# Weighted values of 16 heads on four quarters of the TensorE array, in two PSUM banks

## The chip, the cores and the metric

The kernel runs on one core of a Trainium2 chip. The metric is the device time of one execution in microseconds. TensorE (PE) multiplies, ScalarE (ACT), VectorE (DVE) and GpSimd (POOL) do the rest, and SyncE (SP) issues the transfers.

## What is computed

A decoder of two layers over 64 sequences of 64 tokens, 128 features each, in float32: 4096 tokens, which the kernel holds as 32 tiles of 128 tokens, two sequences to a tile. The parts are, in order: a delta-rule attention, a cross-attention of 16 heads with 8 features, six layers of local attention and feed-forward, then a causal attention of 16 heads with 8 features, a gated cross-attention and a mixture of 16 experts. The step of the change is the weighted sum of values of the two attentions with 16 heads, cut to what matters:

```python
attn = softmax(scores)                       # b, h, q, k: 16 heads, 64 x 64 per sequence
out = jnp.einsum('bhqk,bhkd->bhqd', attn, v) # d = 8
out = out.transpose(0, 2, 1, 3).reshape(B, T, D) @ Wo
```

## The kernel before

**Stages.** The work is in three stages, written by hand with one stream of instructions for each engine. The first ("AB", 32 units, one for each tile) holds the delta rule and the first cross-attention. The middle one ("C1" and "C2") holds the six layers. The last ("DE", 32 units) holds the causal attention, the gated attention and the experts.

**Order.** A unit is cut into phases with short names. `AB_ORDER` and `DE_ORDER` (lines 78 to 96) give for each engine the order of phases in a slot, with a lag: `u5` runs phase `u` of the tile five back. Several tiles are so in work at once, and one slot finishes one tile. `schedule` (line 391) makes each engine's sequence of it; every engine executes its own in that order, and waits on semaphores that count the phases of the others. In the first stage TensorE's slot is V b1 s O u a2 o b2 T w a3 b3 G a4 D b4 v x X p1 t q Z a1 W y p0 J, where the phases of one slot belong to different tiles.

**Phases around the change.** In AB: `J` is the projection of the delta rule into a bank, read by ACT (`J`, `j`) and DVE (`R`, then `Q`). `V` is the last product of the block inverse; DVE `U` waits for it. `O` is the delta rule's output; ACT squares it, DVE `so`, `s2`, POOL `ro` and DVE `N` normalise it, and TensorE `o` transposes that. `a1` to `a4` and `b1` to `b4` are products of sixteen 32x32 blocks; ACT copies `a` out for `b`, DVE subtracts `b` (`d`) and transposes (`t`). `s` makes the scores; the exponentials are transposed by `p0`, `p1` and copied to `PT`. `u` (line 672) calls `weighted16` (line 695), DVE `r` and `n` divide by the sum that stands in each head's ninth column, TensorE `t` transposes, ACT `t` copies to `OT`, and TensorE `y` multiplies by the output weights. In DE the same steps are `u`, `r`, `n`, `t`, and then `w` for the product with `D_Wo`; `h` and `o` with a letter are the two products of an expert, `G` to `C` the weights of the gated attention.

**The weighted values before.** For each of 16 heads and each of the two sequences: one product with a 64x64 stationary operand (the transposed exponentials) and 9 moving columns (8 values and a one). Sequence 0 lies in partitions 0 to 63 and its result goes to partitions 0 to 63, sequence 1 in 64 to 127 and goes there; so two of the array's four 64x64 quarters are used, in turn. All 144 columns of results lie in one bank.

**Banks.** PSUM has eight banks. `take` (line 410) deals them in a rotation in the order of TensorE's phases: each phase gets the next bank, a phase in `AB_PAIRS` or `DE_PAIRS` gets two and begins at an even one (`turn += turn % wide` skips one where needed). Before a phase writes, TensorE waits for the phases that empty the bank's last user (`u.after`); `AB_EMPTIED` (line 142) names them: `"J": ("dve Q",)`, `"u": ("dve n",)`. In the middle stage the rotation has six banks and two are fixed.

Of the kernel before, what the change touches and what calls it, by code (L numbers as in the profile page):

```python
# [146 lines left out]
for _l in "1234":  # L147
    AB_EMPTIED.update({"a" + _l: ("act a" + _l,), "b" + _l: ("dve d" + _l,)})

AB_PAIRS = ("G", "s")  # L150

DE_EMPTIED = {
# [4 lines left out]
}  # L157
for _x in EXPERTS:
    DE_EMPTIED.update({"h" + _x: ("act k" + _x,), "o" + _x: ("dve x" + _x,)})
DE_PAIRS = ("s", "G")  # L160


class Unit:
# [53 lines left out]
def build(nc, din, out, stages=("A", "B", "C", "D", "E", "F"), depth=DEPTH):  # L217
    with ExitStack() as ctx:
# [237 lines left out]
        def pair(u, c):  # L456

            return PS[u.bank["G"] // 2][:, :].rearrange("p (n c) -> p n c", n=2)[:, :, c:c + 256].rearrange("p n (g j) -> p n g j", j=64)

        def program(ab, c1, c2, de, name):  # L460
            for u, ph in schedule(name):
                {"AB": ab, "C1": c1, "C2": c2, "DE": de}[u.kind](u, ph)
# [102 lines left out]
        def _(te):  # L565
            w = Waits(te, sems)

            def mm(o, l, r, start=True, stop=True, check=True):
                return te.matmul(o, l, r, start=start, stop=stop, skip_group_check=not check)  # L569
# [14 lines left out]
            def pe_ab(u, ph):  # L584
# [27 lines left out]
                elif ph[0] == "a":  # L612
                    n = int(ph[1])
                    w.wait_ge(*u.on("dve", f"t{n - 1}"))
                    w.wait_ge(*u.on("pool", "l"))
                    o = blocks16(K, b.BT[:, 128 * n - 128:128 * n], b.D)
                elif ph[0] == "b":
                    w.wait_ge(*u.on("act", "a" + ph[1]))
                    o = blocks16(K, b.E, b.X) if ph[1] < "4" else blocks16(K, b.X, b.E)
                elif ph == "Z":  # L620
                    w.wait_ge(*u.on("dve", "R"))
                    w.wait_ge(*u.on("dve", "d4"))
                    o = blocks16(K, b.E, b.R)
                elif ph == "W":
                    w.wait_ge(*u.on("act", "C"))
                    w.wait_ge(*u.on("act", "Z"))
                    for h in range(4):
                        c = slice(32 * h, 32 * h + 32)
                        for q in (0, 64):
                            o = mm(K[q + 32:q + 64, c], b.CX[q:q + 32, c], b.Z[q:q + 32, c])  # L630
                elif ph == "V":
                    w.wait_ge(*u.on("act", "W"))
                    for h in range(4):
                        c = slice(32 * h, 32 * h + 32)
                        for r in (slice(32, 64), slice(96, 128)):
                            o = mm(K[r, c], b.E[r, c], b.W[r, c])
                elif ph == "O":
                    w.wait_ge(*u.on("dve", "q"))
                    w.wait_ge(*u.on("dve", "U"))
                    for h in range(4):  # L640
                        c = slice(32 * h, 32 * h + 32)
                        for q in (slice(0, 64), slice(64, 128)):
                            o = mm(K[q, c], b.QM[q, 64 * h:64 * h + 64], b.Z[q, c])
                elif ph == "o":
                    w.wait_ge(*u.on("dve", "N"))
                    o = tr(K[:, 0:128], b.ON)
                elif ph == "w":
                    w.wait_ge(*u.on("act", "o"))
                    w.wait_ge("const", 3)
                    o = mm(K[:, 0:128], b.oT, woA[:, :])  # L650
                elif ph == "x":
                    w.wait_ge(f"c{t // 4}", 16)
                    tr(K[:, 128:256], c_sb[:, t, :])
                    w.wait_ge(*u.on("dve", "xn2"))
                    o = tr(K[:, 0:128], b.xnB)
                elif ph == "v":
                    w.wait_ge("k_b", 16 * len(SETS["b"]))
                    w.wait_ge(*u.on("act", "x"))
                    o = mm(K[:, 0:128], b.xc[:, 128:256], T["XWv"][:, :])
                elif ph == "q":  # L660
                    w.wait_ge("k_b", 16 * len(SETS["b"]))
                    w.wait_ge(*u.on("act", "x"))
                    mm(K[:, 0:128], T["XWq"][:, :], b.xc[:, 0:128])
                    o = mm(K[:, 128:256], T["XWk"][:, :], b.xc[:, 128:256])
                elif ph == "s":
                    w.wait_ge(*u.on("act", "q"))
                    o = scores(u.bank[ph], b.qT, b.k4, 512)
                elif ph[0] == "p":
                    w.wait_ge(*u.on("act", "e" + ph[1]))
                    for i in range(4):  # L670
                        o = tr(K[:, 128 * i:128 * i + 128], b.P[int(ph[1])][:, 128 * i:128 * i + 128])
                elif ph == "u":
                    for m in ("v", "p0", "p1"):
                        w.wait_ge(*u.on("act", m))
                    o = weighted16(K, b.PT, b.V9)
                elif ph == "t":
                    w.wait_ge(*u.on("dve", "n"))
                    o = tr(K[:, 0:128], b.On)
                elif ph == "y":
                    w.wait_ge(*u.on("act", "t"))  # L680
                    o = mm(K[:, 0:128], b.OT, T["XWo"][:, :])
# [10 lines left out]
                        o = mm(half(bank[k + g // 2][par:par + 64, :], bb), qT[r, 64 * bb:64 * bb + 64], half(km[r, :], bb))  # L692
                return o

            def weighted16(K, PT, V):
                for h in range(16):
                    c = 128 * (h % 4) + 64 * (h // 4 % 2)
                    for q in (slice(0, 64), slice(64, 128)):
                        o = mm(K[q, 9 * h:9 * h + 9], PT[h // 8][q, c:c + 64], V[q, 9 * h:9 * h + 9])
                return o  # L700

            def pe_bank(u, ph):
# [105 lines left out]
            def pe_de(u, ph):  # L808
# [22 lines left out]
                elif ph == "u":  # L831
                    w.wait_ge(*u.on("dve", "v"))
                    for m in ("p0", "p1"):
                        w.wait_ge(*u.on("act", m))
                    o = weighted16(K, b.PT, b.V9)
                elif ph == "t":
                    w.wait_ge(*u.on("dve", "n"))
                    o = tr(K[:, 0:128], b.On)
# [70 lines left out]
        def _(se):  # L909
# [21 lines left out]
            table("natural_log_exp_and_others")  # L931
            w.wait_ge("k_a", 16 * len(SETS["a"]))

            def act_ab(u, ph):
                b, sm = ab_bufs(u), ab_bufs(u).sm
                K = bank[u.bank[{"j": "J", "C": "G", "D": "G"}.get(ph, ph)]] if ph[0] != "e" else None
# [18 lines left out]
                elif ph[0] == "a":  # L955
                    o = copy(b.X, K[:, 0:128])
                elif ph == "Z":
                    o = copy(b.Z, K[:, 0:128])
                elif ph == "W":
                    for q in (slice(32, 64), slice(96, 128)):  # L960
                        o = copy(b.W[q, :], K[q, 0:128])
                elif ph == "O":
                    o = act(b.SQ[:, 0:128], K[:, 0:128], ACT.Square)
                elif ph == "o":
                    o = copy(b.oT, K[:, 0:128])
                elif ph == "x":
                    o = copy(b.xc, K[:, 0:256])
                elif ph == "v":
                    w.wait_ge("const", 2)
                    o = copy(b.V9[:, :].rearrange("p (h d) -> p h d", d=9)[:, :, 0:8], K[:, 0:128].rearrange("p (h d) -> p h d", d=8))  # L970
                elif ph == "q":
                    w.wait_ge("k_b", 16 * len(SETS["b"]))
                    copy(b.qT, K[:, 0:128])
                    for i in range(4):
                        o = act(b.k4[:, 128 * i:128 * i + 128], K[:, 128:256], ACT.Copy, scale=T["hm8"][:, i:i + 1])
                elif ph[0] == "p":
                    o = copy(b.PT[int(ph[1])], K)
                elif ph == "t":
                    o = copy(b.OT, K[:, 0:128])
                o.then_inc(u.name("act", ph, sems), 1)  # L980

            def act_c1(u, ph):
# [90 lines left out]
            def act_de(u, ph):  # L1073
# [19 lines left out]
                elif ph in ("p0", "p1"):  # L1093
                    o = copy(b.PT[int(ph[1])], K)
                elif ph == "t":
                    o = copy(b.oT, K[:, 0:128])
                elif ph == "xc":
                    w.wait_ge("k_d", 16 * len(SETS["d"]))
                    copy(b.xc, K[:, 0:256])
# [45 lines left out]
        def _(ve):  # L1145
# [20 lines left out]
            def dve_ab(u, ph):  # L1166
# [86 lines left out]
                    w.wait_ge(*u.on("dve", f"s{n}"))  # L1253
                    o = red(sm[:, 3, 8 * n:8 * n + 8], g64(b.P[n]), ALU.max)
                elif ph == "r":
                    o = ve.reciprocal(sm[:, 4, 0:16], K[:, 0:144].rearrange("p (h d) -> p h d", d=9)[:, :, 8])
                elif ph == "n":
                    w.wait_ge(*u.on("dve", "r"))
                    o = tt(b.On.rearrange("p (h d) -> p h d", d=8), K[:, 0:144].rearrange("p (h d) -> p h d", d=9)[:, :, 0:8],
                           bc(sm[:, 4, 0:16], 8), ALU.mult)  # L1260
                o.then_inc(u.name("dve", ph, sems), 1)

            def newton(u, o, a, t, i):
# [125 lines left out]
            def dve_de(u, ph):  # L1389
# [59 lines left out]
                elif ph in ("c0", "c1"):  # L1449
                    o = ts(b.P[int(ph[1])], bank[u.bank["s"] + int(ph[1])], 20.0, -20.0, ALU.min, ALU.max)  # L1450
                elif ph == "r":
                    o = ve.reciprocal(sm[:, 4, 0:16], K[:, 0:144].rearrange("p (h d) -> p h d", d=9)[:, :, 8])
                elif ph == "n":
                    w.wait_ge(*u.on("dve", "r"))
                    o = tt(b.On.rearrange("p (h d) -> p h d", d=8), K[:, 0:144].rearrange("p (h d) -> p h d", d=9)[:, :, 0:8],
                           bc(sm[:, 4, 0:16], 8), ALU.mult)
                elif ph == "w":
                    w.wait_ge(*u.on("pool", "bo"))
                    o = stt(x, K[:, 0:128], 0.5, x, ALU.mult, ALU.add)
# [312 lines left out]
```

## Time and profile before

| | us |
|---|---|
| median of 3 runs | 4253.59 (4252.46 to 4254.8) |
| the profiled execution | 4263.92 |
| its span, first to last instruction | 4262.1 |
| TensorE busy | 4071.3 (96%) |
| ScalarE busy | 3488.6 (82%) |
| VectorE busy | 3291.7 (77%) |
| GpSimd busy | 2653.4 (62%) |
| mean granted TensorE clock | 0.965 |

The times of phases below come from the profiled execution, which took 10.3 us (0.24%) more than the median. Busy is the time in which at least one instruction of the engine was in work; overlapping ones count once. Weight loads (PEld) and products (PE) are separate rows of TensorE; every float32 product appears as two records of each. The granted clock is 1.00 at 2.4 GHz and 0.50 at 1.2 GHz, so a mean between them says how the stretch was divided.

### The profile page before, as it was taken

To read this page: it belongs to the slowest core of one execution; us is meant where nothing else is said; L and a number is where in the kernel's file an instruction comes from. 1 tells how busy PE (TensorE), PEld (TensorE's weight loads), DVE (VectorE), ACT (ScalarE), POOL (GpSimd) and SP (SyncE) were. 2 spreads that over 40 slices of the span, in tenths; PEclk is the share of its full clock that TensorE was granted. 3 is DMA by queue.
4 is the path that set the end of the run, shared out by engine and by line. 5 is a ranking of instruction groups with operands and counts; after the bars stand their busy time and mean duration, and the time that the engine had idled before them with its cause. 6 is when DMAs were issued, how large, how long until landed. Compare 5 with 4: busy or idle time off the path is not lost.

```text
span 4262.1 us, 149492 instructions
## 1 busy us (share of the span) xinstructions
PE 4071.3 (96%) x61520; PEld 3074.8 (72%) x61520; DVE 3291.7 (77%) x9529; ACT 3488.6 (82%) x10059; POOL 2653.4 (62%) x2246
## 2 busy tenths in 40 slices
PE   7999989999999999999999999999999799999999
PEld 5777756666667666667666666676666588888889
DVE  4666578998888888888888888888888467767765
ACT  3455569999999999999999999999999356666665
POOL 3444467887777777777777777777777233333331
PEclk8888889999999999999999999999999789999999
DMA  3000000000000000000000000000000100000000
GB/s 105 4 4 4 4 2 4 5 4 5 30 3 4 4 30 4 4 4 4 30 4 5 5 30 4 5 3 9 27 10 9 30 2 4 4 4 4 4 4 7
DMA packets 65248, 46.34 MB, mean 11 GB/s; under 512 B 29220, under 2 KB 63032, under 8 KB 63800
## 3 DMA queue, kind: packets, MB, share of 16 engines
q1 hardware_dynamic: 64568, 36.78, 3.0%
q8 instruction: 487, 7.98, 0.8%
q14 instruction: 193, 1.58, 0.1%
HBM read 28.48 MB, written 2.10 MB: 7 GB/s over the span
## 4 chain that ended last, share of the span: by engine, by line
PE 41%; ACT 34%; DVE 8%; issue 2%; POOL 0%; ACTq 0%
PE ps L569 34%; ACT BIG L921 15%; ACT BIG L913 12%; PE ps L573 7%; DVE BIG L1149 3%; ACT ps L913 3%; ACT L928 2%; DVE sm L1160 2%; DVE BIG L1154 1%; ACT sm L921 1%; DVE BIG L1157 1%; DVE y_sb L1154 0%; DVE BIG L1153 0%; ACT XS L913 0%; POOL BIG L1591 0%
## 5 line engine op out<-in xcount | busy, mean ns | idle before, releaser
L569 PE MATMUL ps<-WB,BIG 128*128 128x128 f32 (+2 forms) x8576 | 1940.8, 363 | 53.4 <-DVE BIG L1157 47.7
L913 ACT ACTIVATE BIG<-ps 128x512 f32<-128x512 f32 (+6 forms) x3168 | 1518.4, 536 | 461.6 <-PE ps L573 277.8
L1591 POOL TENSOR_TENSOR BIG<-BIG,sm 128x512 f32<-128x512 f32 (+1 forms) x864 | 1221.3, 1425 | 563.6 <-DVE sm L1342 330.0
L569 PEld LDWEIGHTS ps<-WB,BIG 128*128 128x128 f32 (+1 forms) x8576 | 1154.3, 192 | 378.8 <-issue 224.7
L1591 POOL TENSOR_TENSOR BIG<-BIG 128x512 f32<-128x512 f32 x768 | 969.4, 1279 | 146.5 <-DVE BIG L1149 146.5
L1160 DVE TENSOR_REDUCE sm<-BIG 128x8 f32<-128x512 f32 (+3 forms) x1472 | 871.3, 610 | 157.8 <-ACT BIG L921 154.6
L573 PEld LDWEIGHTS ps<-t_ident,BIG 128*128 128x128 f32 x6016 | 731.3, 146 | 325.8 <-issue 167.8
L573 PE MATMUL ps<-t_ident,BIG 128*128 128x128 f32 x6016 | 888.0, 282 | 68.3 <-DVE BIG L1149 28.9
L569 PEld LDWEIGHTS ps<-BIG 64*64 64x64 f32 (+2 forms) x37888 | 617.4, 132 | 336.6 <-ACT BIG L913 78.3
L569 PE MATMUL ps<-BIG 64*64 64x64 f32 (+4 forms) x37888 | 737.2, 226 | 52.7 <-ACT BIG L913 18.6
L1594 POOL TENSOR_TENSOR sm<-sm,halfn 128x1 f32<-128x1 f32 (+2 forms) x336 | 290.5, 871 | 752.0 <-DVE sm L1153 419.8
L921 ACT ACTIVATE BIG<-ps,sm 128x64 f32<-128x64 f32 (+1 forms) x3104 | 694.4, 377 | 14.2 <-DVE sm L1160 10.5
L1149 DVE TENSOR_TENSOR BIG<-ps,rc 128x512 f32<-128x512 f32 x768 | 525.4, 684 | 195.6 <-ACT BIG L921 194.9
L569 PE MATMUL ps<-BIG,WB 128*128 128x128 f32 (+2 forms) x2624 | 597.1, 352 | 2.4 <-ACT BIG L921 1.4
L921 ACT ACTIVATE BIG<-ps 128x512 f32<-128x512 f32 (+1 forms) x832 | 514.7, 628 | 78.9 <-PE ps L569 75.5
L1149 DVE TENSOR_TENSOR BIG<-ps,rs 128x256 f32<-128x256 f32 x1536 | 570.8, 412 | 0.0
L569 PEld LDWEIGHTS ps<-BIG,WB 128*128 128x128 f32 (+1 forms) x2624 | 362.5, 193 | 94.0 <-issue 83.4
L921 ACT ACTIVATE BIG<-ps,t_F_b 128x128 f32<-128x128 f32 x1024 | 324.1, 375 | 83.5 <-PE ps L569 82.7
L1160 DVE TENSOR_REDUCE sm<-ps 128x8 f32<-128x512 f32 (+1 forms) x416 | 266.3, 640 | 72.0 <-PE ps L569 68.4
L913 ACT ACTIVATE ps<-t_bandm 128x512 f32<-128x512 f32 x384 | 266.6, 694 | 0.0
L928 ACT ACT_TABLE_LOAD x187 | 239.9, 1283 | 4.1 <-PEq L1763 0.7
L1157 DVE SCALAR_TENSOR_TENSOR x_sb<-ps,BIG,x_sb 128x128 f32<-128x128 f32 x512 | 177.0, 346 | 77.3 <-PE ps L569 67.4
(119 smaller groups left out, 2913.7 us busy)
## 6 DMA issues: line engine op xcount, KB each, us to landing
WB<-in_Wqkv SPq DMA_DIRECT2D x6, 1536.0 KB, 7.3
XS<-y_sb SPq DMA_DIRECT2D x96, 63.0 KB
y_sb<-in_ctx SPq DMA_DIRECT2D x16, 256.0 KB, 3.2
WB<-in_Wo SPq DMA_DIRECT2D x6, 512.0 KB, 9.0
x_sb<-in_x SPq DMA_DIRECT2D x8, 256.0 KB, 5.2
WB<-in_F_W SPq DMA_DIRECT2D x1, 2048.0 KB, 8.7
WB<-in_F_W SPq DMA_DIRECT2D x8, 256.0 KB, 4.9
out<-x_sb SPq DMA_DIRECT2D x8, 256.0 KB, 2.3
```

Of the source, the lines that this page charges most:

```text
L569: return te.matmul(o, l, r, start=start, stop=stop, skip_group_check=not check)
L573: return te.transpose(o, i, ident[0:n, 0:n])
L913: return se.activation(o, i, ACT.Copy)
L921: return se.activation(o, i, f, **kw)
L928: se.preload_act_table_set(name)
L1149: return ve.tensor_tensor(o, a, b, op)
L1154: return ve.tensor_scalar(o, a, s1, s2, op0, op1)
L1157: return ve.scalar_tensor_tensor(out=o, in0=a, scalar=s, in1=b, op0=op0, op1=op1)
L1160: return ve.tensor_reduce(o, a, AX, op, negate=negate)
L1591: return pe_.tensor_tensor(o, a, b, op)
L1594: return pe_.tensor_tensor(o, a, halfn[:, 0:n], ALU.pow)
```

## The change

`weighted16` takes the bank's number instead of the bank. It goes over eight pairs of heads (`j` and `j + 8`); heads 0 to 7 write to the first bank as before, heads 8 to 15 to the second bank with the two halves of the partitions exchanged, so that the four products of a pair use the four quarters. `u` is added to both lists of pairs. DVE `r` and `n` read the two banks through `weighted`. In the normalised result the columns 64 to 127 (heads 8 to 15) have the two sequences exchanged; after the transpose these are the partitions 64 to 127, and `restore` on ScalarE puts them back with three copies instead of one. The orders of the phases stay.

```diff
-AB_PAIRS = ("G", "s")
+AB_PAIRS = ("G", "s", "u")
-DE_PAIRS = ("s", "G")
+DE_PAIRS = ("s", "G", "u")
+        def weighted(u):
+
+            return PS[u.bank["u"] // 2][:, :].rearrange("p (n c) -> p n c", n=2)[:, :, 0:72].rearrange("p n (h d) -> p n h d", d=9)
...
-                    o = weighted16(K, b.PT, b.V9)
+                    o = weighted16(u.bank[ph], b.PT, b.V9)
...
-            def weighted16(K, PT, V):
-                for h in range(16):
-                    c = 128 * (h % 4) + 64 * (h // 4 % 2)
-                    for q in (slice(0, 64), slice(64, 128)):
-                        o = mm(K[q, 9 * h:9 * h + 9], PT[h // 8][q, c:c + 64], V[q, 9 * h:9 * h + 9])
+            def weighted16(k, PT, V):
+
+                for j in range(8):
+                    c = 128 * (j % 4) + 64 * (j // 4)
+                    for n in range(2):
+                        for bb in range(2):
+                            q, r, v = slice(64 * bb, 64 * bb + 64), slice(64 * (bb ^ n), 64 * (bb ^ n) + 64), 72 * n + 9 * j
+                            o = mm(bank[k + n][r, 9 * j:9 * j + 9], PT[n][q, c:c + 64], V[q, v:v + 9])
...
+            def restore(o, K):
+
+                copy(o[0:64, :], K[0:64, 0:128])
+                copy(o[64:128, 0:64], K[64:128, 64:128])
+                return copy(o[64:128, 64:128], K[64:128, 0:64])
...
-                    o = copy(b.OT, K[:, 0:128])
+                    o = restore(b.OT, K)
...
-                    o = ve.reciprocal(sm[:, 4, 0:16], K[:, 0:144].rearrange("p (h d) -> p h d", d=9)[:, :, 8])
+                    o = ve.reciprocal(sm[:, 4, 0:16].rearrange("p (n h) -> p n h", n=2), weighted(u)[:, :, :, 8])
...
-                    o = tt(b.On.rearrange("p (h d) -> p h d", d=8), K[:, 0:144].rearrange("p (h d) -> p h d", d=9)[:, :, 0:8],
-                           bc(sm[:, 4, 0:16], 8), ALU.mult)
+                    o = tt(b.On.rearrange("p (n h d) -> p n h d", n=2, d=8), weighted(u)[:, :, :, 0:8],
+                           sm[:, 4, 0:16].rearrange("p (n h) -> p n h", n=2).unsqueeze(3).broadcast_to([128, 2, 8, 8]), ALU.mult)
```

The last stage has the same edits for its `u`, `r`, `n` and `t`.

## Rows read from the trace of the kernel before

**Rows 1.** The page: busy time by engine, and the granted clock over 40 slices
```profile
PE 4071.3 (96%) x61520; PEld 3074.8 (72%) x61520; DVE 3291.7 (77%) x9529; ACT 3488.6 (82%) x10059; POOL 2653.4 (62%) x2246
...
PEclk8888889999999999999999999999999789999999
```

**Rows 2.** Table by stretch, first and last stage: us, busy by engine, clock, DMA
```profile
76.07:531.73 455.66, 422.22 (x13333) 342.79 (x13330) 279.77 (x1058) 227.65 (x781) 197.53 (x195) 0.83 0.02 4
...
3500.00:3900.00 400.00, 377.70 (x4458) 352.06 (x4458) 279.66 (x1269) 247.38 (x841) 130.37 (x165) 0.99 0.02 5
```

**Rows 3.** Waits in the first stage, then in the last: total, times, longest
```profile
DVE BIG L1149 <- PE ps L569: 135.8, 51, 5.6
...
PE ps L569 <- DVE BIG L1157: 35.5, 24, 1.9
```

**Rows 4.** Timeline of VectorE in one slot: start, us, operation, idle before
```profile
208.52 0.59 DVE L1149 TENSOR_TENSOR BIG<-BIG,ps 32x128 f32<-32x128 f32 x2 [5.16 <-PE ps L569]
...
212.13 0.69 DVE L1149 TENSOR_TENSOR BIG<-ps,sm 128x256 f32<-128x256 f32 x2
...
212.13 0.41 DVE L1149 TENSOR_TENSOR BIG<-ps,sm 128x256 f32<-128x256 f32 x1
```

**Rows 5.** Timeline of TensorE in the same slot, behind `u`: a2, o, b2, a3, b3
```profile
212.13 0.47 PE L569 MATMUL ps<-BIG 32*32 32x32 f32 x32
212.96 0.45 PE L573 MATMUL ps<-t_ident,BIG 128*128 128x128 f32 x1 [0.36 <-DVE BIG L1149]
213.34 0.65 PE L569 MATMUL ps<-BIG 32*32 32x32 f32 x32
...
215.18 0.65 PE L569 MATMUL ps<-BIG 32*32 32x32 f32 x32
216.23 0.28 PE L569 MATMUL ps<-BIG 32*32 32x32 f32 x4 [0.40 <-ACT BIG L913]
```

**Rows 6.** Timeline of the last stage: oH, w, copy t, r
```profile
3613.02 0.71 PE L569 MATMUL ps<-WB,BIG 128*128 128x128 f32 x4 [1.15 <-DVE BIG L1157]
...
3623.29 0.46 PE L569 MATMUL ps<-t_D_Wo,BIG 128*128 128x128 f32 x2
...
3622.93 0.28 ACT L913 ACTIVATE BIG<-ps 128x128 f32<-128x128 f32 x1 [0.47 <-PE ps L573]
...
3621.19 0.26 DVE L1452 RECIPROCAL sm<-ps 128x16 f32<-128x16 f32 x1 [1.12 <-PE ps L569]
```

**Rows 7.** Timeline of weight loads: O, `u`, `u`, and the middle stage's `y`, `y` with `s`
```profile
209.69 0.54 PEld L569 LDWEIGHTS ps<-BIG 64*64 64x64 f32 x16 [0.39 <-issue]
...
210.16 1.95 PEld L569 LDWEIGHTS ps<-V,BIG 64*64 64x64 f32 x64
...
3619.11 1.94 PEld L569 LDWEIGHTS ps<-V,BIG 64*64 64x64 f32 x64
...
2003.28 1.02 PEld L569 LDWEIGHTS ps<-BIG 64*64 64x64 f32 x64 [0.76 <-ACT BIG L921]
...
2013.58 1.96 PEld L569 LDWEIGHTS ps<-BIG 64*64 64x64 f32 x128 [0.76 <-ACT BIG L913]
```

**Rows 8.** Timeline of TensorE in a slot at full clock: a3 and b3
```profile
232.02 0.45 PE L569 MATMUL ps<-BIG 32*32 32x32 f32 x32
232.88 0.45 PE L569 MATMUL ps<-BIG 32*32 32x32 f32 x32 [0.41 <-ACT BIG L913]
```

**Rows 9.** Table by stretch: three slots, then a part of the last
```profile
227.76:242.49 14.73, 13.20 (x484) 10.53 (x481) 9.92 (x39) 8.21 (x28) 7.09 (x8) 1.00 0.02 3
242.49:258.94 16.45, 15.46 (x484) 12.62 (x480) 10.08 (x39) 8.12 (x28) 7.09 (x8) 0.79 0.02 4
210.16:227.76 17.60, 16.64 (x484) 13.58 (x480) 10.08 (x39) 8.10 (x28) 7.09 (x8) 0.71 0.01 4
...
212.60:223.00 10.40, 9.64 (x234) 7.94 (x238) 6.08 (x24) 4.70 (x15) 4.26 (x5) 0.51 0.01 3
```

**Rows 10.** Timeline of ScalarE: the two copies of phase W
```profile
239.28 0.55 ACT L913 ACTIVATE BIG<-ps 32x128 f32<-32x128 f32 x2
```

More of the change, by code:

```diff
@@ L834, in pe_de @@
                         w.wait_ge(*u.on("act", m))
-                    o = weighted16(K, b.PT, b.V9)
+                    o = weighted16(u.bank[ph], b.PT, b.V9)
                 elif ph == "t":
@@ L1095, in act_de @@
                 elif ph == "t":
-                    o = copy(b.oT, K[:, 0:128])
+                    o = restore(b.oT, K)
                 elif ph == "xc":
@@ L1451, in dve_de @@
                 elif ph == "r":
-                    o = ve.reciprocal(sm[:, 4, 0:16], K[:, 0:144].rearrange("p (h d) -> p h d", d=9)[:, :, 8])
+                    o = ve.reciprocal(sm[:, 4, 0:16].rearrange("p (n h) -> p n h", n=2), weighted(u)[:, :, :, 8])
                 elif ph == "n":
                     w.wait_ge(*u.on("dve", "r"))
-                    o = tt(b.On.rearrange("p (h d) -> p h d", d=8), K[:, 0:144].rearrange("p (h d) -> p h d", d=9)[:, :, 0:8],
-                           bc(sm[:, 4, 0:16], 8), ALU.mult)
+                    o = tt(b.On.rearrange("p (n h d) -> p n h d", n=2, d=8), weighted(u)[:, :, :, 0:8],
+                           sm[:, 4, 0:16].rearrange("p (n h) -> p n h", n=2).unsqueeze(3).broadcast_to([128, 2, 8, 8]), ALU.mult)
                 elif ph == "w":
```

## The prediction

> **What bounds the kernel now.** I read the page first: TensorE is busy 96% of the span and its clock row has 8s in the first six of 40 slices and a 7 and an 8 at the 32nd and 33rd [rows 1]. So the program is three stages with different limits, and the clock is part of them in the first and the last. The table by stretch has these two [rows 2]: in the first stage (28 slots, from one `u` to the next, 455.66 us) TensorE is busy 93% at a mean clock of 0.83; in the last stage TensorE is busy 94% at 0.99. The change touches only the first and the last stage. The middle one runs nothing of it, and its bank rotation (six banks, single turns) keeps the same distances, so I cost it at nothing.
>
> In the first stage the busy share deceives. The list of waits has VectorE waiting 135.8 us for TensorE [rows 3], so they take turns in part. One slot in order of time shows why. VectorE stands idle 5.16 us, gets the product of `V` at 208.52 and then works without a gap for 4.3 us (phases U, ss, d1, y, b, t1, s1, so, be, s2, R, s0, Q, N) until 212.82 [rows 4]. TensorE runs b1, s, O, `u`, a2 beside it and then waits 0.36 us for N before the transpose `o` [rows 5]. So `u` has cover there: even if it were free, `o` would start at 212.96, as now. The slot's length is set by that VectorE chain, by the chain of small steps after it, and by the clock.
>
> The last stage is different: after one wait per slot, ended by the DVE phase C (1.15 us at 3613.02; the waits give 35.5 us in 24), TensorE's phases stand end to end, `u` among them [rows 3, 6]. A shorter `u` is paid out there.
>
> **The change, part by part.**
>
> *The weighted values.* Before, 32 products of 64x64 by 9 columns go to two diagonal quarters; each fp32 product leaves two records, so 64 records take 1.95 us of weight loads (1.94 in the last stage), about 29 ns each [rows 7]. After, the same 64 records cycle through four quarters. The trace has that pattern already: the middle stage's `y` has 64 records of 64x64 on four quarters in 1.02 us, and a `y` with the next tile's `s` behind it 128 in 1.96, so `s` 64 in 0.94 [rows 7]; that is 14 to 16 ns a record though 64 columns move instead of 9. I take 1.02 us, a gain of 0.93 per `u`. If the narrow moving side made a difference the bound above is today's 1.95, below it `s`'s 0.94.
> The Trainium skill has two rules against this. "TensorE: Matmul & The Clock Gate" (section on why 56 ns and not 53.3) says that the start-to-start distance never falls below about 25 ns; by it 64 records need 1.6 us and the gain is 0.35. "TensorEngine Tiling (Array Packing)" (Gotcha 1: PSUM Pressure) says that different row tiles can't use one PSUM bank at once, and the new order sends both row halves to the same bank in pairs. The rows of `s` speak against both: it has the same pairs per bank, at under 15 ns.
>
> *Two banks instead of one.* This is the part that decides. `take` deals banks in turn, and a phase in the list of pairs begins at an even bank. From `J` on the PE order is J, V, b1, s (pair), O, u. If J has bank 1, V has 2, b1 3, s 4 and 5, O 6; `u` as a pair must skip 7 and gets 0 and 1. Bank 1 is J's, and J's bank counts as emptied only by the DVE phase Q (AB_EMPTIED). A slot takes 27 banks, one more for each of the three pairs and two skipped ones, 32 in all, a multiple of 8, so this repeats in every slot. I have 28 slots in which J of a later unit precedes `u` so. Q is the last but one of the VectorE chain: it begins at 212.13 and takes 0.41, so ends at 212.54, while `u` began at 210.16 [rows 4, 7]. N ended at 212.82 and the `o` that waited for it started at 212.96 [rows 4, 5], 0.14 later; so `u`, now at 210.16, will start at 212.66 or so, 2.5 us later, with TensorE idle. Behind it queue a2, o, b2, T, w, a3. a2 starts 1.0 us after that, at 213.7 (now 212.13). From one blocks phase over ScalarE to the next takes 0.86 us at full clock (232.02 to 232.88, a3 to b3) and 1.05 at half (215.18 to 216.23) [rows 5, 8]. So b2 starts at 214.55 to 214.75, now 213.34: 1.2 to 1.4 us late. VectorE's d2 waits for b2 and everything after it follows, so nothing later takes the delay up, and V of the next slot, from which Q is counted, is late by the same. 28 x 1.3 = +36 us.
> The other new bank neighbours release earlier than their users start, by 0.9 us or more in the first stage except b3 (behind n, the two shift together). In the last stage the two banks of `u` are free in time; gT gets one that waits for xL, worth under 0.1 us and hidden in front of `w`.
>
> *The clock.* A slot at full clock lasts 14.73 us, one at mean 0.79 16.45, one at 0.71 17.60 [rows 9]. Mean 0.71 of 17.60 is 10.2 us at the lower level (1.2 GHz), and costs 2.87: 0.28 us per us. Over the 28 slots clock 0.83 gives 155 us at 1.2 GHz, 5.5 a slot, costing 16.27 - 14.73 = 1.54 [rows 2]. All 10.2 us lie in the stretch from 212.60 to 223.00, which is at 0.51 [rows 9]; so the clock fell right behind `u`: there nine-column products and then small blocks with gaps stand, the sparsest work of the slot. The change puts 2.5 us of idle TensorE in front of this. I expect each slot to fall, as the 0.71 ones do: 2.87 - 1.54 = +1.3 at most; with a part of the low time on the idle itself I take +1.1. 28 x 1.1 = +31 us. Bounds: 0 and +37, and, if the low time grew once more by as much as the 0.71 slot has over the 0.79 one (10.2 less 6.9 us), +27 on top.
>
> *The copy in three parts.* One copy of 128x128 takes 0.28 us [rows 6]. Two copies on other partitions than their neighbour's don't overlap: two of 32x128 take 0.55 [rows 10]. A third, narrower one adds 0.1 to 0.2. So 0.65 to 0.75 in place of 0.28, +0.4. In the last stage `w` (t_D_Wo, 3623.29) starts as soon as the copy of 3622.93 is done [rows 6]: the 0.4 stands on the path. In the first stage it stands ahead of X, Z, q, W on ScalarE; where these stand close W, for which V waits, comes later by 0.3 or so, where a gap stands between, by nothing. +0.1 a slot, +3 us (0 to +10).
>
> *VectorE's r and n* read the same number of elements through a pattern with one more level: 0 (0 to +0.1 us each, covered in both stages; `r` has 1.12 us of idle before it in the last [rows 6]).
>
> **Sum.** First stage 36 + 31 + 3 = +70. Last stage: -0.93 + 0.41 = -0.52 a slot for 31 slots, -16; bounds -29 (the copy hidden) to -8. Together +54. The profiled execution took 4263.92 us (span 4262.1), so it would show 4318; the median of the runs is 4253.59, so I forecast **4308 us**.
>
> **The rivals.**
> *The clock keeps its habit.* The bank wait is there, but falls are no more frequent: 36 + 3 - 16 = +23, 4277 us. For: TensorE does the same columns per slot. Against: a falling clock here follows sparse work, and idle is sparser. 0.12.
> *Four quarters bring nothing with nine columns.* `u` stays at 1.95 us by a floor per instruction or a turn-taking at the bank. Then a2 starts 0.93 later still: 28 x 0.93 = +26, and the last stage gives +13 in place of -16: 4308 + 55 = 4363. For: a diagonal product with 32 columns (O: 16 records in 0.54 us) has 27 ns per record against 29 with nine, so columns don't set it, and something else does. Against: the four-quarter rows [rows 7]. 0.07. By the 25 ns that the Trainium skill's page gives, some 60% of that would come.
> *Faster: the clock no longer falls.* Today's falls come right behind the 1.95 us of sparse `u`. If compact products stop the falls, a slot is 14.73 + 1.3 = 16.03 against 16.27: 28 slots bring -7, the copies +3, the last stage -16, in sum -20: 4234 us. It decides from the point at which time at 1.2 GHz is under about 4 us a slot. Against: the idle. 0.05.
> *The change does less than it says*: the wait for Q is met by luck in most slots and gains and losses balance, within 8.5 us of 4253.6. Against: a chain without a gap and a fixed rotation. 0.02.
> My forecast has 0.74.
>
> **How the numbers follow.** Forecast's own bounds: 4277 - 5 below (clock rival and a little of the last stage's gain), above 4308 + 6 (clock at its bound) + 7 (copies) + 8 (the last stage's least) and part of the still longer low time: 4343. That takes in the first rival; the others, 0.14, are outside. The measurement can tell about 0.2%, 8.5 us. Faster by more: 0.05; within: 0.02; slower: 0.93.
>
> **What would show it.** In the first stage: `u` preceded by about 2.5 us of TensorE idle, ended by the DVE phase Q, in nearly all slots; `u` about 1.0 us; the wait before `o` gone; slots of 18 to 19 us, mean clock near 0.72. In the last stage: slots shorter by 0.5 us, `w` waiting for the third copy, the wait for C unchanged. The forecast fails if J's bank is not the one that `u` gets, if Q is reached sooner than 2 us after O, or if the clock stays up.

## The result, and the profile after

The changed kernel takes 4353.57 us (median of 4 runs, 4352.22 to 4357.17), the kernel before 4253.35 beside it (4252.46 to 4254.8): a ratio of 1.0236, interval 1.0223 to 1.025, so 100 us slower. The profiled execution took 4357.17 us, span 4355.4, that is 93 us more than the profiled execution before. It was forecast slower, by 54 us and at most 89.

The page of the profile has TensorE a little busier in us and less busy in share, and a lower clock row in slices 2 to 6, which are the first stage (before: 8s there, [rows 1]):

```profile
PE 4095.9 (94%) x61520; PEld 3084.5 (71%) x61520; DVE 3296.3 (76%) x9529; ACT 3514.2 (81%) x10187; POOL 2653.5 (61%) x2246
...
PEclk8766678999999999999999999999999879999999
```

The table by stretch (us, busy of PE, PEld, DVE, ACT and POOL with counts, granted clock, DMA share, GB/s): the first stage from the first `u` to the 29th, one slot of it, that slot's parts, and 400 us of the last stage.

```profile
76.66:634.60 557.94, 471.63 (x13325) 384.11 (x13326) 279.05 (x1051) 237.20 (x836) 195.31 (x193) 0.68 0.01 3
216.82:236.94 20.12, 17.02 (x476) 13.88 (x477) 10.08 (x39) 8.52 (x30) 7.10 (x8) 0.67 0.02 4
...
214.40:216.80 2.40, 0.11 (x4) 0.00 (x0) 2.40 (x9) 0.28 (x1) 2.28 (x3) 0.85 0.00 0
...
216.85:224.00 7.15, 6.58 (x207) 5.44 (x207) 3.55 (x13) 2.19 (x6) 2.34 (x3) 0.50 0.02 6
224.00:230.00 6.00, 6.00 (x166) 5.32 (x164) 2.44 (x12) 2.94 (x12) 1.83 (x2) 0.52 0.01 4
230.00:236.90 6.90, 4.44 (x128) 3.10 (x118) 4.02 (x15) 3.40 (x13) 2.85 (x3) 0.97 0.01 2
...
3500.00:3900.00 400.00, 369.00 (x4372) 335.27 (x4372) 279.95 (x1261) 250.01 (x854) 135.91 (x172) 0.94 0.01 4
```

The first stage took 455.66 us at a clock of 0.83 [rows 2], now 557.94 at 0.68: all of the loss and more. VectorE's busy time there is the same (279.77 to 279.05), so nothing got longer on the engine that the slot waits for; the time is wait and clock. A mean clock of 0.67 in 20.12 us is 2 x 0.33 x 20.12 = 13.3 us at 1.2 GHz. The parts show where: the clock has already fallen in the 2.40 us in which TensorE has nothing to do ahead of `u` (0.85), and stays at 0.50 through `u` until some 13 us behind its start. Before, the low part began behind `u`, at 212.60, and ended at 223.00 [rows 9]. Over the stage, 15 of the 28 falls begin in the idle ahead of `u` (up to 0.8 us ahead of its start), 10 within 0.6 us behind its start and 3 behind it by 1.7; before, there were 19 falls, 18 of them 2.3 to 4.5 us behind the start of `u`.

The waits of TensorE over the first stage (what waited for what: us in total, times, longest) have a new first row; line 1162 is VectorE's product, of which phase Q is one:

```profile
PE ps L573 <- DVE BIG L1162: 63.2, 27, 2.5
PE ps L573 <- ACT BIG L920: 19.2, 49, 0.6
```

One slot in order of time (start, us, operation, idle before): VectorE from `U` to N, then TensorE's product and weight-load rows around `u`, at half clock, and the product row of `u` in another slot at full clock:

```profile
212.68 0.59 DVE L1162 TENSOR_TENSOR BIG<-BIG,ps 32x128 f32<-32x128 f32 x2 [5.45 <-PE ps L573]
...
216.29 0.69 DVE L1162 TENSOR_TENSOR BIG<-ps,sm 128x256 f32<-128x256 f32 x2
```
```profile
216.85 1.89 PE L573 MATMUL ps<-V,BIG 64*64 64x9 f32 x64 [2.34 <-DVE BIG L1162]
...
213.86 0.54 PEld L573 LDWEIGHTS ps<-BIG 64*64 64x64 f32 x16 [0.39 <-issue]
216.82 1.82 PEld L573 LDWEIGHTS ps<-V,BIG 64*64 64x64 f32 x64 [2.42 <-issue]
...
436.26 1.12 PE L573 MATMUL ps<-V,BIG 64*64 64x9 f32 x64 [2.33 <-DVE BIG L1162]
```

VectorE's chain is as it was [rows 4]: 4.3 us without a gap. O's weight loads end at 214.40, where `u` used to follow at once [rows 7]; now `u` starts at 216.82, 2.42 us later, as Q releases it. That holds in each of the 28 slots (2.28 to 2.61 us, 26 of them 2.41 or 2.42). At full clock `u` takes 1.02 to 1.1 us, at half clock 1.82; of the 28, 20 take over 1.6 us, 5 lie between, where the clock falls inside `u`, and 3 are at full clock.

In the last stage (TensorE, then ScalarE) `u`, the transpose `t`, the copies and `w` are these; [rows 6] and [rows 7] are their like before:

```profile
3723.20 1.12 PE L573 MATMUL ps<-V,BIG 64*64 64x9 f32 x64
...
3725.80 0.38 PE L577 MATMUL ps<-t_ident,BIG 128*128 128x128 f32 x2
3726.02 0.61 PE L573 MATMUL ps<-WB,BIG 128*128 128x128 f32 x4
3726.77 0.49 PE L573 MATMUL ps<-t_D_Wo,BIG 128*128 128x128 f32 x2
```
```profile
3726.11 0.61 ACT L920 ACTIVATE BIG<-ps 64x128 f32<-64x128 f32 x3 [0.47 <-PE ps L577]
```

The three copies take 0.61 us for 0.28, and `w` follows their end by 0.05. From the weight loads of `t` to those of `w` it takes 1.08 us, before 0.75. An ordinary slot went from 26.31 to 25.73 us.

Where the 93 us lie, stretch by stretch in the two traces and in those of the experiments below, each from the start of one `u` to the start of another (32 in each of the two stages); "low" is the time at 1.2 GHz in the stretch. "Middle" goes from the 29th `u` of the first stage to the first of the last, so it holds three slots of the first stage too (40.9 us before, 44.4 after):

| | first stage, `u` 1 to 29 | low | middle | last, `u` 1 to 5 | last, `u` 5 to 32 | low | span |
|---|---|---|---|---|---|---|---|
| before | 455.7 | 157 | 2827.8 | 100.3 | 728.3 | 17 | 4262.1 |
| after | 557.9 | 358 | 2830.6 | 100.5 | 716.4 | 24 | 4355.4 |
| e1_last_only | 452.1 | 140 | 2823.6 | 99.4 | 718.8 | 24 | 4244.0 |
| e2_pair_only | 587.4 | 369 | 2828.0 | 100.2 | 726.1 | 17 | 4393.5 |
| e9_pair_free | 464.8 | 157 | 2830.7 | 100.0 | 721.5 | 10 | 4266.5 |
| e3_other_banks | 466.6 | 184 | 2832.3 | 99.7 | 702.0 | 7 | 4249.5 |
| e4_filled_wait | 566.7 | 92 | 2836.9 | 99.9 | 705.0 | 10 | 4360.8 |
| e5_fill_ten | 502.8 | 92 | 2833.9 | 99.7 | 702.7 | 10 | 4291.3 |
| e6_before_filled | 452.9 | 89 | 2836.7 | 100.7 | 711.0 | 0 | 4252.4 |
| e7_banks_filled | 467.3 | 68 | 2831.5 | 97.5 | 706.2 | 10 | 4250.5 |
| e8_last_banks | 452.9 | 147 | 2837.0 | 99.2 | 685.1 | 0 | 4227.0 |

From the last `u` of the first stage to the first of the last, where the code is all but the same in all of them, the time differs by up to 11 us from one execution to another (2783.0 to 2794.1). The first stage of one and the same code took 455.7, 452.1 and 452.9 us (before, e1_last_only, e8_last_banks). So a difference of some 10 us between two spans says nothing, and one of 4 us in the first stage neither; a stage must be read by itself.

### The profile page after: what moved, and what is told of

Same layout as the page of the kernel before. It is cut to its first block, busy times and chain, and to the rows that moved or that the text cites. A ratio compares the mean times of both kernels' runs of the same rounds, so it can differ in the third digit from the quotient of the medians.

```text
span 4355.4 us, 149619 instructions
## 1 busy us (share of the span) xinstructions
PE 4095.9 (94%) x61520; PEld 3084.5 (71%) x61520; DVE 3296.3 (76%) x9529; ACT 3514.2 (81%) x10187; POOL 2653.5 (61%) x2246
## 4 chain that ended last, share of the span: by engine, by line
PE 39%; ACT 34%; DVE 7%; issue 2%; POOL 0%; ACTq 0%
PE ps L573 32%; ACT BIG L928 15%; ACT BIG L920 13%; PE ps L577 7%; DVE BIG L1162 3%; ACT ps L920 3%; ACT L935 2%; DVE sm L1173 2%; DVE BIG L1167 1%; ACT sm L928 1%; DVE BIG L1170 1%; DVE BIG L1166 0%; DVE y_sb L1167 0%; ACT XS L920 0%; POOL BIG L1604 0%
## 5 line engine op out<-in xcount | busy, mean ns | idle before, releaser
L920 ACT ACTIVATE BIG<-ps 128x512 f32<-128x512 f32 (+6 forms) x3296 | 1541.2, 523 | 535.2 <-PE ps L573 267.0
L577 PEld LDWEIGHTS ps<-t_ident,BIG 128*128 128x128 f32 x6016 | 742.4, 148 | 317.4 <-issue 166.1
L577 PE MATMUL ps<-t_ident,BIG 128*128 128x128 f32 x6016 | 904.7, 286 | 61.2 <-DVE BIG L1162 23.2
L573 PEld LDWEIGHTS ps<-BIG 64*64 64x64 f32 (+2 forms) x37888 | 639.9, 136 | 345.9 <-issue 103.3
L573 PE MATMUL ps<-BIG 64*64 64x64 f32 (+4 forms) x37888 | 762.6, 231 | 54.6 <-ACT BIG L920 23.0
L1162 DVE TENSOR_TENSOR BIG<-BIG,ps 128x128 f32<-128x128 f32 (+1 forms) x192 | 54.7, 285 | 261.8 <-PE ps L573 260.3
```

The source lines that it names most:

```text
L577: return te.transpose(o, i, ident[0:n, 0:n])
L920: return se.activation(o, i, ACT.Copy)
L1162: return ve.tensor_tensor(o, a, b, op)
```

## The experiments

Theory: the second bank of `u` is `J`'s, so `u` waits for Q; that wait costs once by itself and once more through the clock, and the last stage gains. Rivals: four-quarter products cost the first stage something themselves; the three copies do; the clock's part is only a companion, and the wait does it all.

**One stage alone.** The lines of the first stage are taken back, the last one keeps the change:

```diff
-AB_PAIRS = ("G", "s", "u")
+AB_PAIRS = ("G", "s")
...
-                    o = weighted16(u.bank[ph], b.PT, b.V9)
+                    o = old16(K, b.PT, b.V9)
...
-                    o = restore(b.OT, K)
+                    o = copy(b.OT, K[:, 0:128])
```

> The change in the last stage alone; the first stage is as before. Theory (the loss comes whole from the first stage, where u waits for the DVE phase Q): the last stage keeps its slot of 25.73 us against 26.31, so 4241 us (4236 to 4247). Rival (part of the loss is in the last or the middle stage, from new bank neighbours): above 4253.

Measured: 4237.0 us (4233.25 to 4245.78), ratio 0.9945 (0.9924 to 0.9966). The first stage is back at 452.1 us. The last stage alone makes the kernel faster, so the loss is the first stage's entirely.

**The pair alone.** The kernel before, with `u` in the first stage's list of pairs; products and copy stay, the second bank is dealt and not written:

```diff
-AB_PAIRS = ("G", "s")
+AB_PAIRS = ("G", "s", "u")
```

> The kernel before with one word more: u takes a pair of banks in the first stage and uses only the first of them; products, reads and copy as before. Theory (the bank that it shares with J makes the loss): u waits 2.4 us for Q in each slot, the clock falls for about 13 of 20 us, slots of 20 to 21 us, 4353 to 4375 us. Rival (four-quarter products or the copy in three parts make the loss): below 4275.

Measured: 4390.05 us (4385.02 to 4395.3), ratio 1.0304 (1.0282 to 1.0326). One entry in a list, with no instruction more, costs 136 us: more than the whole change. Its weight loads around `u`, and the row of that stretch in the table (clock third from the end):

```profile
206.93 3.52 PEld L569 LDWEIGHTS ps<-V,BIG 64*64 64x64 f32 x64 [2.35 <-issue]
210.47 0.51 PEld L569 LDWEIGHTS ps<-BIG 32*32 32x32 f32 x32
```
```profile
206.93:210.45 3.52, 3.49 (x64) 3.52 (x64) 0.95 (x3) 0.00 (x0) 1.33 (x2) 0.50 0.02 5
```

The same wait, and behind it the old `u` at 0.50, which takes 3.52 us and not 1.95, in 14 of the 28 slots. I had priced `u` at its full-clock duration; in these slots it isn't one, which fits with a run 15 us above what was expected. With four quarters `u` takes 1.82 us there, 1.7 less, and the first stage is 29.5 us shorter (557.9 for 587.4). So behind the wait the new products are a gain, and the wait is the loss.

**The wait away, the rest kept.** The whole change, but `u` in the first stage passes over two more banks, so that its pair is 2 and 3 in place of 0 and 1:

```diff
-            turn += turn % wide
+            turn += turn % wide + 2 * (ph == "u" and u.stage == "ab")
```

> The change whole, but u's pair in the first stage begins two banks further, so that its banks are those of V and b1, emptied by U and d1 before u starts, and not p0's and J's. Theory: no wait before u, the wait before o grows from 0.4 to 1.3 us instead, slots of 16.3 us or a little more as before, 4242 us (4230 to 4262). Rival (products and copies themselves cost in the first stage): above 4300.

Measured: 4250.61 us (4241.58 to 4265.9, 10 runs), ratio 0.999 (0.9972 to 1.0008). The first stage is 466.6 us, 91 less than after. Its weight loads of `u`, a2 and `o`:

```profile
239.95 0.14 PEld L573 LDWEIGHTS ps<-V,BIG 64*64 64x64 f32 x2
...
240.00 1.04 PEld L573 LDWEIGHTS ps<-V,BIG 64*64 64x64 f32 x62
242.13 0.34 PEld L573 LDWEIGHTS ps<-BIG 32*32 32x32 f32 x32 [1.09 <-DVE BIG L1170]
242.75 0.14 PEld L577 LDWEIGHTS ps<-t_ident,BIG 128*128 128x128 f32 x1 [0.27 <-DVE BIG L1162]
```
```profile
241.40 0.68 DVE L1170 SCALAR_TENSOR_TENSOR BIG<-ps,t_causm 128x512 f32<-128x512 f32 x1
```

`u` starts with O's last loads and is over in 1.04 us; but then a2 waits 1.09 for VectorE, and `o` starts 2.8 us after `u`, as before [rows 5, 7]. What `u` saves in this stage is idle time. The wait of a2 is for a bank once more: two banks further in the rotation it gets one of `s`'s, which VectorE's `s1` empties (the last row, done at 242.08). It moves neither `o` nor b2, which start 2.80 and 3.06 us after `u` (before 2.78 and 3.04). The run was expected at 4242 and lies inside its range; the stage isn't as long as before's, but 11 us longer, with 184 us at 1.2 GHz for 157.

**The pair without the wait.** To see whose those 11 us are: the pair-only kernel with the same passing over of two banks, so old products, old copy, no wait for Q.

```diff
-AB_PAIRS = ("G", "s")
+AB_PAIRS = ("G", "s", "u")
...
-            turn += turn % wide
+            turn += turn % wide + 2 * (ph == "u" and u.stage == "ab")
```

> e2_pair_only with the pair two banks further, as in e3_other_banks; products, reads and copies as before. Theory (of the 137 us that e2 lost all is the wait and its clock): 4247 to 4258 us, no wait before u. Rival (a pair more in the rotation costs by itself, through skipped banks): above 4270. Beside e3 (4250.6) and e1 (4237.0) it tells whether e3's first stage lost to its pair or to its products and copies.

Measured: 4269.64 us (4263.02 to 4286.08, 10 runs), ratio 1.0039 (1.0025 to 1.0053), 12 us above what was expected and at the edge of the rival that a pair more costs something by itself. The first stage takes 464.8 us, within 2 us of the 466.6 of the whole change on the same banks. So products and copies together change the first stage there by no more than such stages differ anyway. But the two stages don't lose in the same way. With the whole change the full-clock slots are those of before (14.6 to 14.9 us) and the low time is 27 us longer, worth 7.6 us at 0.28. Here the low time is that of before, the nine full-clock slots take 14.6 to 15.6 us (mean 14.9, before 14.7), and three slots take 19.6 to 20.4 us with 10.2 to 13.7 us low, for which 14.7 and 0.28 us per us give 17.6 to 18.5. TensorE's waits have a row that before's hardly has (0.5 us once):

```profile
PE ps L569 <- issue: 4.4, 8, 1.2
```

These eight idle times lie between two products of 32x32 blocks, none of them at a wait for a semaphore. What ended them the trace doesn't say, and it stays open.

**The wait filled.** The whole change with its wait; but between O and `u` TensorE multiplies the identity by itself into columns of `u`'s bank that nobody reads, first 18 and then 10 times. These products are no part of the computation. If the clock is a cost of its own, the kernel gets faster by added work.

```diff
                 for v, e, m in u.after[ph]:
-                    w.wait_ge(*v.on(e, m))
+                    if m != "Q" or ph != "u":
+                        w.wait_ge(*v.on(e, m))
+                if ph == "u":
+                    for i in range(18):      # second kernel: range(10)
+                        mm(bank[u.bank[ph]][:, 128:256], ident[:, :], ident[:, :])
+                for v, e, m in u.after[ph]:
+                    w.wait_ge(*v.on(e, m))
```

> The change whole, and 18 products of 128x128 without use (36 records of 128 columns, about 2 us at 2.4 GHz) written to u's first bank ahead of the wait for Q; u overwrites nothing that is read, its result is the same. The wait stays. Theory (of the loss about a third is the wait, two thirds the clock that it lets fall): granted clock near 1.0 in the first stage, slots of 16.1 us in place of 20.2, 4245 us (4238 to 4280). Rival (the wait itself costs the 100 us, the clock is a by-product): 4335 to 4365.

> As e4_filled_wait, with 10 useless products instead of 18. In e4 a record of these took 117 ns, so 36 held TensorE 4.2 us, 1.8 longer than the wait; 20 records are 2.3 us, just the wait of 2.4. Theory (about a third of the loss is the wait, the rest the clock): slots at full clock of 16.4 to 16.5 us, first stage 465 to 485 us in place of 558, 4262 to 4285 us. Rival (the wait itself costs the 100 us): 4335 to 4365.

Measured: with 18, 4353.26 us (4346.47 to 4362.61), ratio 1.0216 (1.0193 to 1.0238), far from the 4245 expected: the 36 records took 4.2 us, 1.8 more than the wait, so `u` came late by that, and a slot at full clock took 18.2 to 19.4 us. The low time had fallen from 358 to 92 us all the same. It was expected that the 36 records would take about 2 us; they leave TensorE 117 ns apart. With 10, 4283.02 us (4277.16 to 4293.14), ratio 1.0077 (1.0051 to 1.0103): 70 us faster than after, by nothing but work whose result is thrown away (in the traces 55 us of it lie in the first stage and 14 in the last, which runs the same code in both). Its rows, fill, `u` and b2 of one slot and the table of the slot before (clock 1.00), of this one (0.83), and of the stage (0.91):

```profile
174.83 2.50 PE L573 MATMUL ps<-t_ident 128*128 128x128 f32 x20
177.26 1.12 PE L573 MATMUL ps<-V,BIG 64*64 64x9 f32 x64
...
179.25 0.45 PE L573 MATMUL ps<-BIG 32*32 32x32 f32 x32 [0.24 <-ACT BIG L926]
```
```profile
158.53:174.83 16.30, 14.77 (x501) 12.05 (x497) 10.03 (x39) 8.46 (x30) 7.09 (x8) 1.00 0.02 4
174.83:194.59 19.76, 17.57 (x501) 14.42 (x497) 10.19 (x39) 8.47 (x30) 7.09 (x8) 0.83 0.01 3
76.50:579.30 502.80, 452.31 (x13889) 370.63 (x13886) 281.31 (x1058) 238.28 (x837) 197.35 (x195) 0.91 0.02 4
```

The fill reaches from 174.83 to 177.26, 2.43 us, exactly the wait. So the first row is a slot with the wait and without the clock: 16.30 us (14 such slots, 16.26 to 16.53 with a mean of 16.38, and one of 17.33) against 14.73 [rows 9]. The wait by itself, with what little the new products and copies add, costs some 1.65 us a slot, 28 x 1.65 = 46 us. After's slot of 20.12 us has 13.3 us low, so (20.12 - 16.30) / 13.3 = 0.29 us per us, the price that before's slots have. Of the first stage's 102 us the other 56 are the clock, and (358 - 157) x 0.28 gives the same 56. That rules out the rival that the wait does it all: with the wait kept, the first stage is 55 us shorter.

The stage itself missed its 465 to 485 us. Its 92 us at 1.2 GHz cost (502.8 - 28 x 16.38) / 92 = 0.48 us each: its 13 falls begin 6.0 to 8.4 us behind the start of `u`, in other phases than before's. So 0.28 is the price of the stretch around and right behind `u`. Whether the other phases make a us at 1.2 GHz dearer, or the fill, which leaves TensorE less idle time in the slot, isn't shown.

**Fillers in other places.** If low time costs 0.28 us per us, before's 157 us are worth 44 us. Two kernels put useless products ahead of phases that wait, one on the kernel before, one on the whole change with `u` on the other banks:

```diff
+                for i in range({"o": 1, "b3": 2, "a4": 1}.get(ph, 0)):      # second kernel: "o": 4, "b3": 1, "a4": 1
+                    mm(bank[u.bank[ph]][:, 0:128], ident[:, :], ident[:, :])
```

> The kernel before with useless 128x128 products in waits of the first stage: one ahead of o, two ahead of b3, one ahead of a4, each 0.23 us at 2.4 GHz, written to the phase's own bank and overwritten. Theory (the clock falls for sparse work and costs 0.28 us for each us at 1.2 GHz, 157 us of them in before's first stage): clock near 1.0, first stage 415 to 430 us in place of 456, 4212 to 4230 us. Rival (idle and order of work set the slots, the clock follows without cost): 4254 or above, since the products can only delay.

> e3_other_banks with useless products: four ahead of o, one ahead of b3, one ahead of a4. With u short and unhindered, o waits 1.2 us for N; four products (0.94 us) fit. Theory: clock near 1.0 in the first stage, slots of 14.8 us, first stage 415 to 425 us, and the last stage's gain of 12: 4200 to 4215 us. Rival (the shorter u brings nothing even so and the fill delays): 4240 or above.

Measured: 4244.06 us (4234.17 to 4254.21, 10 runs), ratio 0.9986 (0.9971 to 1.0002), and 4240.05 us (4235.58 to 4255.25), ratio 0.9982 (0.9965 to 0.9999). Both missed what was expected, by 14 and 25 us from the nearer end. The table rows of the first stage say why: the clock did rise, to 0.90 and 0.93 (before 0.83, [rows 2]), but the length didn't follow.

```profile
77.30:530.20 452.90, 437.71 (x13557) 354.64 (x13554) 281.83 (x1058) 227.89 (x781) 197.77 (x195) 0.90 0.02 4
```
```profile
74.70:542.00 467.30, 417.77 (x13671) 333.85 (x13669) 281.94 (x1058) 236.56 (x837) 197.48 (x195) 0.93 0.02 4
```

In the first, a slot at full clock takes 14.9 to 15.5 us for 14.7. In the second b2 starts 3.6 to 5.0 us after `u`, in place of 3.0 to 3.3 in e3_other_banks, behind the fillers, and eight records of them take 1.16 us at full clock and 2.08 at half. The four products ahead of `o` counted on a wait of 1.2 us for N; but a2 takes 1.0 us of it with its wait for `s1`, and `o` itself waits 0.3. Filling paid here in the 2.4 us ahead of `u`, where TensorE waits as long as the filler lasts, and not in waits of 0.3 us.

**The last stage's own bank waits.** With the last stage alone changed, one wait a slot is left there, that for C [rows 3]. Two phases pass over two banks:

```diff
+            turn += {"oH": 2, "p1": 2}.get(ph, 0) * (u.stage == "de")
             turn += turn % wide
```

> e1_last_only (change in the last stage alone), and in the last stage the rotation skips two banks ahead of oH and two ahead of p1. oH then no longer gets the bank of G that the DVE phase C empties; in the trace of before it waits 1.15 us for that in each slot, and C's value itself is wanted only three phases later. Theory (the wait for C is a bank wait like the one of u, of the rotation's making): oH and hL go ahead, slots shorter by 0.6 to 0.9 us, 4210 to 4222 us. Rival (the wait only moves to p1 or ct, which need POOL's and C's results): 4234 to 4240 as e1.

Measured: 4226.67 us (4224.9 to 4228.74), ratio 0.9932 (0.9906 to 0.9958), 5 us above what was expected and below what the rival gives; it is the fastest kernel of this study by its median, though its interval overlaps that of e1_last_only. The waits of TensorE from 3500 to 3900 us, of after and then of this kernel:

```profile
PE ps L573 <- DVE BIG L1170: 18.5, 13, 1.9
PE ps L577 <- POOL BIG L1604: 5.0, 2, 2.8
```
```profile
PE ps L578 <- ACT BIG L936: 7.4, 16, 0.5
```
```profile
3500.00:3900.00 400.00, 388.63 (x4759) 355.70 (x4759) 300.69 (x1355) 271.22 (x934) 138.64 (x173) 1.00 0.02 5
```

The wait for C was a wait for a bank. A slot is 25.36 us instead of 25.73 (two of 25.5 and 25.6), those of 26.45 and 28.1 are gone, the clock is 1.00, and 27 slots take 685.1 us for the 718.8 of e1_last_only. Of these 34 us only 17 show between the two spans, since the middle took 13 us more and what follows the last `u` 3, and 10 between the medians; why is open.

A kernel with four quarters and one bank was not tried. There the two row halves would write to the same partitions of one bank, and no run here shows whether that is safe.

## Why the prediction was wrong in size and right in mechanism

*Cover in the first stage, density in the last: right.* Without the wait the faster `u` brings the first stage nothing (e3_other_banks against e9_pair_free: 466.6 and 464.8 us; `o` starts 2.80 us after `u`, before 2.78); the last stage gains 0.58 us in an ordinary slot.

*`u` at 1.02 us: right at full clock* (1.02 to 1.09), so 16 ns per record where the Trainium skill ("TensorE: Matmul & The Clock Gate", on why 56 ns and not 53.3) has about 25 ns as the least distance. And two row halves in pairs on each bank run at that rate, where the Trainium skill ("TensorEngine Tiling (Array Packing)", Gotcha 1: PSUM Pressure) says that they can't use one bank at once. The measurement decides in both. But the term was taken at full clock, while behind the wait 20 of 28 `u` run at half clock wholly or nearly so (1.71 to 1.83 us).

*The bank: right in place and length, small in price.* `u` waits for Q in all 28 slots, by 2.42 us (2.5 forecast). In e5_fill_ten b2 starts 4.4 us after O's last load (179.25 against 174.83), in before's slots at full clock 3.0, so 1.4 later (1.2 to 1.4 forecast). The slot grows by 1.65 in place of 1.3 + 0.1 with the copies: 46 us in place of the 39 of both. Where the other 0.25 us come from is open.

*The clock: the step that failed.* I let each slot fall as before's worst slots do, 10.2 us low, and capped the term at +1.3 with 1.1 chosen. That took the place and length of the low stretch from the kernel before, while the change moves what goes ahead of them: the fall begins about where `u` starts, in 15 slots in the idle ahead of it, and no longer behind it, so the stretch holds `u` as well and lasts 13.3 us in the slot shown. Such a slot pays (13.3 - 5.5) x 0.29 = 2.3 us, and the mean of the 28 is 2.0, not 1.1. By the stage: 56 us where 31 stood. The case was in my bounds (the low time growing once more, +27), and I left most of it out of the range; with the whole of it the upper end would have been 4356 and held the time. The expected slots of 18 to 19 us at 0.72 were 20.2 at 0.67.

*The copies: near.* 0.61 us for 0.28, +0.33 on the path in the last stage (0.41 forecast). In the first stage they and the products together make 2 us when nothing waits for Q (3 forecast), less than the 4 us by which stages of the same code differ.

*The last stage: -12 in place of -16.* The ordinary slot gave more than forecast (0.58 for 0.52). But slots come in three lengths: before, of 27, 14 took 26.3 to 26.5 us, 8 took 27.0 and 5, with a fall of the clock, 28.7; after, 13 took 25.7, 7 took 26.4 and 7 took 28.1. So two slots more fell. In e3_other_banks, whose last stage is the same, 2 fell and the stretch takes 702.0 us for 716.4: that share is scatter between executions, not the change's; 27 ordinary gains of 0.58 are 16 us, the forecast.

*The sum.* First stage +102 for +70, last stage -12 for -16, middle +3 for 0: 93 in the profiled executions, 39 more than forecast. The +3 belong to the change too: the three slots of the first stage behind the 29th `u`, which no term of mine counted, grew from 40.9 to 44.4 us. The median moved by 100 since before's profiled execution lay 10 us above its median and after's 4.

*The rivals.* The clock's keeping its habit and the clock's no longer falling both fell by the 358 us low; four quarters bringing nothing fell by the 1.02 us; the wait being met by luck in most slots fell by the 28 waits in 28 slots.

## What to carry to other kernels

Where buffers are dealt in rotation, one entry wider is a new set of neighbours for every phase behind it: before such a change, list for each phase whose buffer it gets and when that one is emptied, in the trace of the kernel before. One false wait in front of a cheap phase cost here 46 us by itself and 56 through the clock, and skipping two banks took nearly all of it back, though it gave another phase a wait of 1.0 us for a bank. When a change puts idle time ahead of a sparse phase, price the low-clock stretch anew, with the phase inside it at its half-clock duration, rather than from the slots of the old kernel.

## What the runs showed of the hardware

- Weight loads of 64x64 with nine moving columns, per record: on two quarters 30 ns at 2.4 GHz and 55 at 1.2 (1.95 and 3.52 us for 64); on four quarters 16 and 28 (1.02 and 1.82 us). At 2.4 GHz the records start in groups, of two on two quarters and of four on four, 7 ns apart within a group and 55 to 59 ns from group to group.
- Useless work in a wait can shorten a kernel: 20 records of 128x128 in the 2.4 us ahead of `u` took it from 4353.57 to 4283.02 us; 36 records, which overshoot the wait by 1.8 us, brought nothing (4353.26 us).
- A us at 1.2 GHz had no fixed price: 0.28 to 0.29 us where the falls began around or right behind `u`, 0.48 in e5_fill_ten, where they began 6.0 to 8.4 us behind its start.
- The records of 128x128 products of float32 start 117 to 122 ns apart at 2.4 GHz (36 in 4.2 us, 20 in 2.43), which sets how much a fill of given length holds.
- Three copies out of PSUM by ScalarE, cut by partitions, take 0.61 us for 0.28 in one. The second, on other partitions than the first, starts when the first is over; the third, on the same as the second, starts 0.12 us after it.
- From the last `u` of the first stage to the first of the last, all but unchanged code took 2783.0 to 2794.1 us in eleven traces; no cause was found.
